# Two causal attentions on one core: the range flag made earlier or on TensorE, PSUM banks handed over in two steps, the head's splits reordered, four heads in one narrow exponential

## What is computed

```python
x = ln(x + attn0(x));  x = ln(x + ffn0(x))   # ffn0: mxfp4-quantised matmul
x = ln(x + attn1(x));  x = ln(x + ffn1(x))   # ffn1: 8 experts, top 2, and a shared one
# attn0: 16 query heads of 16 dims in 4 groups that share k and v
q, k = rope(q / (|q| + 1e-6) * alpha * sqrt(16)), rope(k / (|k| + 1e-6))
# attn1: 16 heads with k and v of their own, rope, no normalisation
attn = softmax(where(causal, q @ k.T / sqrt(16), -inf)) @ v;  out = attn @ Wo + bo
```

## Time and profile before

| what | value |
| --- | --- |
| median of 3 runs | 835.37 us (835.29 to 838.1) |
| the profiled execution, its own time | 839.44 us |
| its span | 837.4 us |
| TensorE busy | 733.7 us, 88% of the span |
| ACT busy | 403.3 us, 48% |
| DVE busy | 401.6 us, 48% |
| POOL busy | 167.9 us, 20% |
| mean granted TensorE clock | 0.934 |
| first scores of layer 0 / of layer 1 | 98.31 us / 413.10 us |
| exponentials (L1255) | 384 instructions, 278.9 us |

### The profile page before, as it was taken

One profiled execution on the slowest core, in us unless ns is written; L12 is line 12 of the kernel. 1 busy time (PEld: TensorE's weight loads), 2 busy tenths in 40 slices (PEclk: granted clock), 3 DMA queues, 4 the chain that ended last, 5 costly groups with the idle time before them and its releaser, 6 DMA issues.

```text
span 837.4 us, 10933 instructions
## 1 busy us (share of the span) xinstructions
PE 733.7 (88%) x3784; PEld 328.5 (39%) x3784; DVE 401.6 (48%) x989; ACT 403.3 (48%) x590; POOL 167.9 (20%) x188
## 2 busy tenths in 40 slices
PE   5987399999996668668299999999999999999996
PEld 2546022222332534324122222323438438448345
DVE  3688333333377779763123333345452662552524
ACT  1243488999784352543278888886111111121110
POOL 0012324432334121210223422331200200000000
PEclk9996599999999789878699999998999999999998
DMA  8301233333200000012415554471000000000000
GB/s 291 87 1 31 51 54 56 56 56 52 52 2 1 1 0 14 0 32 47 69 35 87 83 85 81 80 171 59 1 0 1 0 26 1 25 0 0 25 1 25
DMA packets 31602, 36.37 MB, mean 43 GB/s; under 512 B 7664, under 2 KB 19757, under 8 KB 31389
## 3 DMA queue, kind: packets, MB, share of 16 engines
q1 hardware_dynamic: 31541, 35.60, 20.9%
HBM read 12.74 MB, written 2.10 MB: 18 GB/s over the span
## 4 chain that ended last, share of the span: by engine, by line
PE 59%; DVE 16%; ACT 9%; issue 7%; SPq 5%; POOL 1%; DMA 1%; DVEq 0%; ACTq 0%; POOLq 0%
PE ps L1738 16%; PE ps L1196 12%; PE ps L1179 10%; PE ps L1762 8%; ACT probs L1255 6%; SPq L913 2%; SPq L920 2%; PE ps L1408 2%; DVE stats L285 2%; PE ps L635 1%; PE ps L428 1%; PE ps L1748 1%; PE ps L659 1%; DVE norm_small L258 1%; PE ps L673 1%
## 5 line engine op out<-in xcount | busy, mean ns | idle before, releaser
L1255 ACT ACTIVATE probs<-ps 128x1024 f32<-128x1024 f32 (+3 forms) x384 | 278.9, 837 | 71.5 <-PE ps L1179 70.2
L1179 PE MATMUL ps<-ops_mem 99*128 99x512 bf16 (+3 forms) x768 | 167.7, 337 | 30.9 <-issue 23.0
L1196 PE MATMUL ps<-probs,vstat 128*32 128x512 f32 (+3 forms) x1536 | 167.1, 508 | 6.0 <-DVE raw L1115 3.2
L1738 PE MATMUL ps<-ops_mem,parts_mem 128*128 128x512 f32 x320 | 147.2, 606 | 1.2 <-DVE probs L1790 1.2
L1273 POOL TENSOR_SCALAR_AFFINE_SELECT probs<-probs 128x512 f32<-128x512 f32 x128 | 86.9, 681 | 226.0 <-ACT probs L1255 225.1
L1179 PEld LDWEIGHTS ps<-ops_mem 99*128 99x128 bf16 x768 | 56.4, 99 | 188.6 <-ACT probs L1255 111.9
L1115 DVE COPY raw<-ps 128x512 f32<-128x512 f32 x32 | 22.1, 692 | 177.3 <-PE ps L1196 177.1
L1684 ACT ACTIVATE ops_mem<-ps 128x512 f32<-128x512 f32 x40 | 23.9, 597 | 143.1 <-PE ps L1738 143.1
L1738 PEld LDWEIGHTS ps<-ops_mem,parts_mem 128*128 128x128 f32 x320 | 58.9, 191 | 68.7 <-issue 66.1
L1762 PE MATMUL ps<-parts_mem,probs 128*128 128x256 f32 x320 | 70.5, 380 | 0.0
L1762 PEld LDWEIGHTS ps<-parts_mem,probs 128*128 128x128 f32 x320 | 60.3, 190 | 8.4 <-issue 0.5
(11 more groups left out here) (175 smaller groups left out, 721.2 us busy)
## 6 DMA issues: line engine op xcount, KB each, us to landing
ops_mem<-parts_mem SPq DMA_DIRECT2D x288, 64.0 KB
yT<-in_xT SPq DMA_DIRECT2D x4, 512.0 KB, 6.9
xres<-in_x SPq DMA_DIRECT2D x1, 2048.0 KB, 13.7
ops_mem<-parts_mem SPq DMA_DIRECT2D x48, 32.0 KB
out<-ops_mem SPq DMA_DIRECT2D x3, 512.0 KB, 2.9
rope<-in_rope SPq DMA_DIRECT2D x1, 1024.0 KB, 6.9
parts_mem<-in_wg SPq DMA_DIRECT2D x2, 512.0 KB, 4.9
parts_mem<-in_wu SPq DMA_DIRECT2D x2, 512.0 KB, 7.4
```

The source lines that it names most:

```text
L1179: last = nc.tensor.matmul(ps[:, 2 * (n % 3) + h % 2, 0:CH - lo], kT[0:KDIM, buf, h if kh == GH else 0, kt * P:(kt + 1) * P], qT[0:KDIM, bu ...
L1196: last = nc.tensor.matmul(ps[32 * h:32 * h + 32, av_bank(i, c), lo:CH], vstat[:, i % 2, kt, h if kh == GH else 0, :], probs[:, s % PRING, ...
L1255: nc.scalar.activation(probs[:, s % PRING, 2 * pair:2 * pair + 2, 0:CH - lo], ps[:, 2 * (n % 3):2 * (n % 3) + 2, 0:CH - lo], ACT.Exp, scal ...
L1738: last = nc.tensor.matmul(ps[:, 4 + 2 * (e % 2) + m, :], w, xT[:, kk, :], start=kk == 0, stop=kk == 1)
```

## The change

1. **Flag of layer 0.** `decide` does the two DVE instructions at u = 2 of the head's loop. The register load and the branch stay where they were.
2. **Flag of layer 1.** Memset, two reductions and POOL's reduction over the partitions go. DVE takes one maximum per partition behind the last `norms`; TensorE turns that column into a row (a matmul with the identity); DVE reduces the row to two numbers, multiplies and compares, on one partition.
3. **Banks in two steps.** `banks_free` is now a generator: before the first step's scores TensorE waits for the readers of banks 0 to 3 alone, and for the last `less_hi` only ahead of the second step.
4. **Head.** The transposed factors go to bank 4 and not to half of bank 7; the squares of the last two units are summed (`lengths`) ahead of the chunk's transposes; on DVE `normalised(u)` comes ahead of `less_hi(u - 1)`, on ACT `keep_hi(u)` ahead of `keep_mid(u - 1)`.
5. **Narrow steps.** Where 256 or 128 queries are left, the scores of all four heads go into one pair of banks, side by side, and one exponential takes them. An item has 20 exponentials and not 24; the semaphores count accordingly.

```diff
+        def decide(dve):
+            nc.vector.tensor_reduce(guard[:, 0:1], alpha[:, 0:HEADS], AX.X, ALU.max, apply_absolute_value=True
+                                    ).then_inc(s_longest[0], 1)
+            dve.wait_ge(s_longest[0], 1)
+            nc.vector.tensor_scalar(flag[:, :], guard[:, 0:1], BOUND, None, ALU.is_gt).then_inc(s_flag[0], 1)
...
                 def factors(m):
                     pe.wait_ge(s_ysp, m + 1)
+                    if m > 0:
+                        pe.wait_ge(s_rest, NTL * m - 2)
+                    else:
+                        pe.wait_ge(s_w4k, 1)
...
+                    if NU <= u < NU + 2:
+                        lengths(u - 2)
                     if 0 <= u - LATER < NU:
                         if (u - LATER) % NTL == 0:
                             factors((u - LATER) // NTL)
...
-                    if 0 <= u - 2 < NU:
+                    if 2 <= u < NU:
...
+                    if 0 <= u - LATER < NU:
+                        keep_hi(u - LATER)
                     if 0 <= u - LATER - 1 < NU:
                         keep_mid(u - LATER - 1)
-                    if 0 <= u - LATER < NU:
-                        keep_hi(u - LATER)
...
+                    if 0 <= u - LATER < NU:
+                        normalised(u - LATER)
                     if 0 <= u - LATER - 1 < NU:
                         less_hi(u - LATER - 1)
-                    if 0 <= u - LATER < NU:
-                        normalised(u - LATER)
...
             def banks_free(pe):
+                pe.wait_ge(s_a_read, len(ORDER))
+                pe.wait_ge(s_sq, NU)
+                yield
                 pe.wait_ge(s_rest, NU)
-                pe.wait_ge(s_a_read, len(ORDER))
+                yield
...
+        TOGETHER = [GH if 2 * width(s) <= CH else 2 for s in range(NS)]
+        EXPS = [sum(GH // n for n in TOGETHER[:s]) for s in range(NS + 1)]
+        NEXP = EXPS[NS]
...
             def _(pe):
-                pe.wait_ge(s_flag, 1)
+                if layer == 1:
+                    pe.wait_ge(s_longest[1], 1)
+                    nc.tensor.matmul(ps[0:1, 7, 0:P], guard[:, 0:1], ident[:, :], start=True, stop=True
+                                     ).then_inc(s_over, 1)
+                pe.wait_ge(s_flag[layer], 1)
                 large = pe.value_load(flag[0:1, 0:1], min_val=0, max_val=1)
...
-                    for pair in range(2):
-                        n = 2 * s + pair
-                        if i * 2 * NS + n >= 3:
-                            pe.wait_ge(s_exp, i * 2 * NS + n - 2)
-                        for h in (2 * pair, 2 * pair + 1):
-                            last = nc.tensor.matmul(ps[:, 2 * (n % 3) + h % 2, 0:CH - lo],
+                    for j in range(GH // TOGETHER[s]):
+                        n = i * NEXP + EXPS[s] + j
+                        if n >= 3:
+                            pe.wait_ge(s_exp, n - 2)
+                        for h in range(TOGETHER[s] * j, TOGETHER[s] * (j + 1)):
+                            o = h % 2 * (CH - lo) if TOGETHER[s] == GH else 0
+                            bank = 2 * (n % 3) + (h // 2 if TOGETHER[s] == GH else h % 2)
+                            last = nc.tensor.matmul(ps[:, bank, o:o + CH - lo],
```

More of the change, by code:

```diff
@@ L586, in build @@
         YN_COUNT, YN_HALF = 18, 11
+        s_longest, s_flag = ([sem(f"{name}{layer}") for layer in range(2)] for name in ("s_longest", "s_flag"))
+        def decide(dve):
[3 more added lines that the diff above has]
+            nc.vector.tensor_scalar(flag[:, :], guard[:, 0:1], BOUND, None, ALU.is_gt).then_inc(s_flag[0], 1)
         def head():
@@ L667, in lengths @@
                         pe.wait_ge(s_n2_read, m)
-                    if n == 2 and m > 0:
-                        pe.wait_ge(s_ynk, m)
                     lo, w = (8 * n, 8) if n < 2 else (HEADS, NG)
@@ L947, in maxima @@
         def maxima(layer, ops):
-            s_longest = sem(f"s_longest{layer}")
             if layer == 1:
                 s_over, s_guard = sem("s_over"), sem("s_guard")
-            s_flag = sem(f"s_flag{layer}")
             s_row = loop_sem(f"s_row{layer}")
@@ L1203, in values_product @@
                         last.then_inc(s_av, 1)
-                banks_free(pe)
+                free = banks_free(pe)
+                next(free)
                 ops.there(pe, 0)
                 scores(0, 0)
+                next(free)
                 scores(0, 1)
```

70 lines of the change are left out of this document (33 added, 37 removed).

## The result

The changed kernel took 829.6 us (median of 7 runs, 827.46 to 832.34) beside 835.71 for the kernel before (7 runs, 834.07 to 838.56): a ratio of 0.9916, 95% interval 0.9893 to 0.9939. That is faster, by 7 us as the ratio counts it (the medians differ by 6.1) and not by the 11.7 of the forecast, and 829.6 lies above the range that ended at 828.2. It was timed twice more as an experiment, in later sets of runs: 0.9885 (0.9851 to 0.9919) and 0.987 (0.9837 to 0.9903). The mean of the three, weighted by their intervals, is 0.9897 (0.988 to 0.9914), a gain of 8 to 9 us; taken off 835.37 it would give 826.8, inside the range. So part of the miss in time is this first measurement, and the step that failed has to be read from the rows.

A forecast was written before the change was run, and what follows sets the result against it. The chain was held 59% by TensorE, 16% by DVE; gains lay in attention starts, the head's end and a stall per item. 4.3 + 1.3 + 6.1 = 11.7 us off 835.37 gave 823.7 us, range 820.6 to 828.2.

The forecast's parts named there:

- Narrow steps: Attention items: step 2's matmuls run through, 0.22 us per item in items 1 to 6 of layer 0, 1.3 us.
- the start of layer 0: End of head: with the flag early, first scores come at 94.0 for 98.31, 4.3 us earlier; bounds 3.0 and 5.3.
- The meetings of DVE with POOL's low parts: Head, last factors: unit 5's low part falls on DVE's factors, and one more meeting costs 0.95 us.
- `less_hi(8)` ahead of the last spreading: End of head: unit 11's spreading waits for `less_hi(8)`, done at 88.65, and ends by 89.3, not about 88.0.
- The tail's gain: End of head: DVE and ACT overlap, so the last low part ends at 94.2 against 95.04, 0.85 us.
- Layer 1: Between the layers: flag 6.4 us earlier, first scores at 406.7; third stack 6.05 us earlier, so 6.1 us won.
- (a): Rival: SP's queue eats the early start, layer 0's third stack late or layer 1's stacks longer; 827.4 us, chance 0.10.
- (b): Rival: the branch costs more where it now lies, perhaps an instruction fetch meeting `stack(0)`; 2 us, 825.7, chance 0.07.
- (c): Rival: ACT's saved time in the exponentials comes through, layer 0 wins up to 3 us more; 820.8 us, chance 0.08.
- (d): Rival: slower, as the four-head exponential starts late in the narrow steps; 20.8 us on top, 844.5, chance 0.03.

The follow-up runs named there:

- exp4_only: The kernel before with the four-head exponentials alone; ratio 0.996 of the kernel before.
- no_reorder: The changed kernel with the head's old order on all engines, the rest of the change kept; ratio 0.9875 of the kernel before.
- flag0_only: The kernel before with layer 0's flag made early and its banks given in two steps, alone; ratio 0.9946, 4.5 us.
- load_early: The changed kernel with the lengths put back and TensorE's load of layer 0's flag at unit 4; 3.01 us from last spreading to first scores.
- again2: The changed kernel once more, nothing edited, on the chip of the last four runs; ratio 0.987 of the kernel before.

## Why the forecast was too good

**The step that failed** is the first one of the start of layer 0: that `spread` of unit 6 would come at 72.9 as before, that DVE would finish `less_hi(5)` by 74.75 and could start the last factors there, "because the last squares are already summed". That they are summed early is exactly what TensorE pays for: it takes its instructions in order, and the lengths of unit 11, put ahead of the transposes, wait for ACT's square of that unit. Transposes, spreading, DVE's normalisation and factors stood behind that wait. Spreading of unit 6 came at 77.1 to 78.4 us in four profiles of this head, DVE's last factors at 80.23, the last spreading ended at 93.3 to 94.6 and not at 89.3. I followed DVE's order through and left TensorE's old times standing. At equal clock this step measured 2.1 to 2.2 us. The clock, which fell to half at 61 us in the first profile and not at 67, took 2 to 2.5 us more, and the sum had no term for its course in the head: exp4_only and no_reorder have the old head with such a fall, and their last spreading ended at 90.11 and 90.55 for 88.04. The first scores gained -0.7, -0.2 and 0.8 us in three profiles, for 4.3 forecast. Of the two causes the order is the change's own, shown by rows and not by a time of its own; the clock fell early in old and new orders alike, so its part of the miss is not shown to be the change's, and looks like chance. With DVE's and ACT's order at 1.6 us for 1.3, the three make up 5.0 of the 5.3 us by which the last spreading (94.64) came later than the 89.3 forecast.

**What held in that term.** The flag alone is worth what I gave the whole (flag0_only: 4.5 us in time). Load and branch took 4.36, 4.44 and 4.17 us behind the last spreading, for 4.87. The meetings of DVE with POOL's low parts came as reckoned (1.16 us for a 0.24 us instruction at 81.13, just behind a low part's start at 81.04). `less_hi(8)` ahead of the last spreading cost 1.2 us for 1.3 (88.75 to 91.41 with the lengths back, 86.58 to 88.04 before). The tail's gain is there as well: from the spreading of unit 9 to the end of the last low part 7.7 us with the lengths back, 8.5 before, so 0.8 for 0.85.

**A limit that I did not name**: DVE's own flag load and branch hold its copy of item 0's values, and with them TensorE's step 2 (1.15 us at 97.09 in flag0_only). An early start of TensorE was never worth its full length. The landing of the first stack, which I had 3 us ahead of the scores, came 1.6 us ahead of them with the change, because the low part of unit 5 came at 81.04 and not at 75.45.

**Narrow steps**: 0.22 us an item were forecast, 1.3 us in all. TensorE's wait in step 2 went, as said, and 0.14 to 0.18 us arrived at the next value product; POOL's mask of step 1, behind ACT's exponentials of steps 0 and 1, took nearly all of it back, 0.04 to 0.06 us an item stayed. I had taken the work behind it to be TensorE's alone up to step 4. That this form is still worth 1.4 to 3.3 us in three timed pairs is more than this mechanism gives; where the forecast's 1.3 us lies near the timed gain, it is luck. ACT's busy time in the exponentials fell by 3.1 us (278.9 to 275.8, 0.05 for each one saved, for 0.07 reckoned), so a gain of 3 us would need all of it to come through.

**Layer 1** was right: 6.76 us from low part to scores for 6.4, first scores 405.71 for 406.7 (0.6 us of that because the last low part came earlier), third stack 6.28 us earlier for 6.05, capped by the zeros as said, and 5.7 us for the flag alone in time, for 6.1. No POOL instruction is left between the last low part and the scores; ahead of it, in the middle part, there still are some, so the forecast's "no POOL instruction between the layers" was too wide.

**The range.** It was said to take in the bounds of the terms, and does not: 5.3 + 4.2 + 6.8 = 16.3 us would be 819.1, below its 820.6. Nothing hangs on it here, since the miss is at the other end.

**The rivals.** (a) fell, though the changed kernel does not test it, as its early start did not come: the third stack of layer 0 starts at 121.42, behind zeros that come 3 us later than the 118.29 of the earlier trace rows, and item 2 starts at 138.81 for 138.72 with no wait for a DMA. Flag0_only does test it: there the third stack is issued until 132.03, and item 2 starts 4.0 us early, at 134.69, with no such wait. Nor do layer 1's stacks lengthen: item 1 to item 7 takes 120.6 us for 121.0. (b) fell: the branch cost less, not more; and for the Trainium skill's rule (Runtime: NRT & Kernel Launch, Instruction fetch mechanics, a taken branch outside the prefetched window forces a fetch) load_early bounds what is left for it on TensorE at 3 us of the 4.4. That time passes behind the branch agrees with the rule (2.83 us on DVE); that it is a fetch no run here shows. (c) is not decided, as the narrow steps show. (d) fell: TensorE's wait for ACT behind a four-head exponential was 0.16 us.

## What to carry to other kernels

When instructions are moved ahead on an engine that takes them in order, price what stands *behind* their waits, not only who gets their result sooner; and carry new times through all engines, not through the one in view. When a wait is taken away from a start, look for the other engines' waits of the same kind (here DVE's own flag load and branch) and for the transfer that was hidden under it. Take the flag, the register load and the branch as three parts that can be placed apart.

## What was unexpected of the hardware

TensorE's granted clock in the head is not the same from one execution to the next. In the window from 60 to 70 us the changed kernel and, below it, the one with the lengths back read (columns as in the earlier trace rows):

```profile
60.00:70.00 10.00, 10.00 (x27) 5.48 (x25) 8.01 (x21) 3.69 (x8) 1.15 (x1) 0.51 0.00 0
```

```profile
60.00:70.00 10.00, 10.00 (x32) 5.22 (x31) 7.32 (x19) 4.19 (x9) 1.19 (x2) 0.69 0.01 2
```

The clock is 0.51 in the one and 0.69 in the other, though up to the lengths of unit 9 at 67.6 us the two have the same instructions, and 0.89 before. again2, the changed kernel once more, reads 0.67. This was 1 to 2 us of the start of layer 0 in either direction, as much as the parts that were to be told apart. What helped was to compare only stretches at one clock, counted from a row ahead of the edit: three profiles of the changed head then agree to 0.01 us (33.12 us to the end of the last spreading).

Four DMAs of zeros for three partitions each take 3.1 us to issue, and the last landed 6.37 us behind the start of its issue (422.49, above), where the row of ones took 2.88 (94.50). They are worth moving ahead of what waits for them.

A branch that jumps over a part that is never run took long as well: from the branch to DVE's next instruction it was 2.83 us in flag0_only and 3.04 in load_early, three times the load and register work ahead of it.
